# Attention in a fused transformer block: weighted values of two steps one behind the other, with four probability buffers

## The reference

```
x = x + 0.5 * moe(layernorm(x))          # 32 experts, top 8, capacity 128
x = x + attention(layernorm(x))
x = x + 0.5 * moe(layernorm(x))
# attention: 2 batches x 1024 tokens x 128 features, 16 heads of 8, rotary part of 32 common to the heads
c_kv = x @ W_kv_down
scores = (q . k + q_rope . k_rope) / sqrt(8 + 32), causal
attn = softmax(scores) @ v;   out = attn @ W_o
```

## Time and profile before

| | us |
|---|---|
| median of 3 runs | 605.45 (604.97 to 607.55) |
| profiled execution | 603.74 |
| its span | 601.7 |
| TensorE busy | 534.7 (89%) |
| VectorE busy | 425.6 (71%) |
| ScalarE busy | 259.8 (43%) |
| GpSimd busy | 89.3 (15%) |

### The profile page before, as it was taken

How to read it: one execution, slowest core, us unless ns; L and a number is a source line. 1 busy time by engine, 2 the same in 40 slices (tenths; PEclk the granted TensorE clock), 3 DMA queues, 4 the chain that set the end, 5 groups by cost and what they waited for, 6 DMA issues and landing times.

```text
span 601.7 us, 11027 instructions
## 1 busy us (share of the span) xinstructions
PE 534.7 (89%) x3522; PEld 332.9 (55%) x3546; DVE 425.6 (71%) x1423; ACT 259.8 (43%) x430; POOL 89.3 (15%) x208
## 2 busy tenths in 40 slices
PE   6869999969798999999999999999987875899995
PEld 2746767744464554555555555555533543577784
DVE  6966878774776776867678686767800895698973
ACT  2733212234544456465545646554577331121212
POOL 2500000011601121121212112121222140000000
PEclk9979999998997999999999999999999986899998
DMA  9964100000151000000000000000000620000002
GB/s 200 186 224 126 37 1 3 1 3 2 60 221 54 2 26 28 27 23 12 24 27 26 28 28 23 12 23 27 0 2 1 172 65 1 1 3 1 2 3 70
DMA packets 25094, 26.70 MB, mean 44 GB/s; under 512 B 6704, under 2 KB 18576, under 8 KB 25040
## 3 DMA queue, kind: packets, MB, share of 16 engines
q1 hardware_dynamic: 24176, 25.63, 15.1%
q10 hardware_dynamic: 864, 0.36, 0.2%
HBM read 17.04 MB, written 8.78 MB: 43 GB/s over the span
## 4 chain that ended last, share of the span: by engine, by line
PE 64%; DVE 23%; issue 6%; ACT 5%; DMA 1%; DVEq 0%; SPq 0%; POOL 0%; ACTq 0%
PE ps L1520 13%; PE ps L1585 12%; PE ps L1558 10%; PE ps L1236 7%; PE ps L1335 5%; PE ps L1320 4%; DVE onehot L880 3%; DVE mxh L1078 3%; PE ps L1516 2%; DVE summed L1075 2%; DVE place L954 2%; PE ps L1348 2%; DVE xn L804 2%; ACT probs L717 2%; DVE stats L780 1%
## 5 line engine op out<-in xcount | busy, mean ns | idle before, releaser
L717 ACT ACTIVATE probs<-ps 128x1024 f32<-128x1024 f32 (+2 forms) x192 | 148.2, 809 | 118.0 <-PE ps L1558 117.9
L1078 DVE TENSOR_REDUCE mxh<-ps 128x1 f32<-128x512 f32 (+2 forms) x176 | 117.4, 689 | 48.1 <-PE ps L1520 46.0
L1520 PE MATMUL ps<-Kst,Qst 120*128 120x512 f32 (+3 forms) x384 | 132.7, 412 | 7.0 <-DVE mxh L1078 3.9
L1520 PEld LDWEIGHTS ps<-Kst,Qst 120*128 120x128 f32 x384 | 67.1, 192 | 64.1 <-DVE mxh L1075 23.3
L1558 PE MATMUL ps<-Qst,Kst 121*128 121x512 f32 (+3 forms) x384 | 96.1, 356 | 1.9 <-ACT probs L717 1.7
L1075 DVE CUSTOM_DVE_ANT_0 summed<-ps,maskf 128x384 f32<-128x384 f32 (+1 forms) x128 | 76.0, 620 | 22.3 <-PE ps L1520 20.5
L1236 PE MATMUL ps<-onehot,xp 128*128 128x512 bf16 (+1 forms) x250 | 70.0, 407 | 17.1 <-DVE onehot L880 15.9
L490 POOL TENSOR_SCALAR_AFFINE_SELECT probs<-probs 128x256 f32<-128x256 f32 x128 | 52.1, 407 | 222.1 <-ACT probs L717 221.5
L1585 PE MATMUL ps<-probs,Vst 128*32 128x512 f32 (+3 forms) x768 | 82.4, 501 | 1.2 <-POOL probs L490 1.2
L1558 PEld LDWEIGHTS ps<-Qst,Kst 121*128 121x128 f32 x384 | 67.2, 191 | 22.6 <-ACT probs L717 7.3
L880 DVE TENSOR_SCALAR onehot<-iotab,posm 128x128 bf16<-128x128 bf16 (+1 forms) x352 | 63.0, 254 | 2.3 <-issue 2.0
(11 more groups left out here) (179 smaller groups left out, 607.2 us busy)
## 6 DMA issues: line engine op xcount, KB each, us to landing
wgn<-in_L_ffn_gate_up_proj SPq DMA_DIRECT2D x8, 384.0 KB, 6.2
guT_d<-gus SPq DMA_DIRECT2D x6, 384.0 KB, 3.1
gus<-guT_d SPq DMA_DIRECT2D x6, 384.0 KB, 6.2
Kst<-kn_d SPq DMA_DIRECT2D x28, 64.0 KB
Qst<-qn_d SPq DMA_DIRECT2D x28, 64.0 KB
wdn<-in_L_ffn_down_proj SPq DMA_DIRECT2D x8, 192.0 KB, 6.7
dnT_d<-dns SPq DMA_DIRECT2D x6, 192.0 KB, 3.5
dns<-dnT_d SPq DMA_DIRECT2D x6, 192.0 KB, 7.4
```

The source lines that it names most:

```text
L717: e.activation(probs[n % RING][:, 2 * b:2 * b + 2, lo:BANK], ps[:, 2 * b:2 * b + 2, lo:BANK], ACT.Exp, scale=SCALE).then_inc(probs_ready, 1)
L1078: e.tensor_reduce(to, s.rearrange("p (q k) -> p q k", k=w), AX.X, ALU.max).then_inc(mx_ready, 1)
L1520: ins = e.matmul(ps[:, bank, i * w:(i + 1) * w], Qst[p][h][0:ROWS, column(b, jt * P):column(b, jt * P) + P], Kst[p][h][0:ROWS, column(b, o ...
```

## The change

The weighted values are no longer issued in each step: in the odd steps those of the even step before and of the step itself are issued one directly behind the other (`BURST = 2`). The third and fourth quarters of the share stay in every step, behind them. There are four probability buffers (`PRING`). Three of them lie where `nh` and `nl` lie, so ScalarE waits before its first exponential until all stores of these are done. `SHARE` is set anew; its sum stays 38, and its entries for steps 1, 2, 3, 4, 8 and 10 change.

```diff
--- before.py
+++ after.py
@@ -80,7 +80,9 @@
 
 
 
-SHARE = [4, 3, 4, 3, 4, 3, 4, 4, 3, 3, 3, 0]
+SHARE = [4, 4, 3, 4, 3, 3, 4, 4, 2, 3, 4, 0]
+BURST = 2
+PRING = 2 * BURST
 LASTU = max(n for n in range(NS) if SHARE[n])
 LATE = OPENS[1]
 TH = BANK // P
@@ -231,8 +233,11 @@
         ord_ = sb("ord", [P, 4, 4], F32, att)
 
 
-        nh = [sb(f"nh{u}", [P, BANK], F32R, att) for u in range(NB)]
-        nl = [sb(f"nl{u}", [P, BANK], F32R, att) for u in range(NB)]
+        parting = ExitStack()
+        nh = [sb(f"nh{u}", [P, BANK], F32R, parting) for u in range(NB)]
+        nl = [sb(f"nl{u}", [P, BANK], F32R, parting) for u in range(NB)]
+        parting.close()
+        probs = [sb(f"probs{p}", [P, 4, BANK], F32, att) for p in range(PRING - 1)]
         ckvT = sb("ckvT", [D, N], F32, att)
 
         pre = ExitStack()
@@ -244,7 +249,7 @@
         ll = [sb(f"ll{s}", [P, BANK], F32R, pre) for s in range(2)]
         pre.close()
 
-        probs = [sb(f"probs{p}", [P, 4, BANK], F32, att) for p in range(RING)]
+        probs += [sb(f"probs{p}", [P, 4, BANK], F32, att) for p in range(PRING - 1, PRING)]
         oS = [sb(f"oS{j}", [P, BANK], F32, att) for j in range(2)]
         att.close()
         attn = xn
@@ -486,7 +491,7 @@
                     lo = kt * P - j * BANK
                     for b in range(B):
                         e.wait_ge(probs_ready, pair * 2 * NS + 2 * n + b + 1 + RING)
-                        block = probs[n % RING][:, 2 * b:2 * b + 2, lo:lo + P]
+                        block = probs[n % PRING][:, 2 * b:2 * b + 2, lo:lo + P]
                         e.affine_select(block, block, [[0, 2], [1, P]], ALU.is_ge, zero, base=0, channel_multiplier=-1).then_inc(masked, 1)
                     if n == DIAG[2] and pair + 1 < NPAIR:
                         stage_values(pair + 1, 1 - p)
@@ -707,14 +712,17 @@
 
 
             def pair_step(pair, p, half, first=False):
+                if first:
+                    for u in range(2 * NC):
+                        e.wait_ge(nope_stored[u], 32)
                 for n, (j, kt) in enumerate(STEPS):
                     lo = max(0, kt * P - j * BANK)
                     for b in range(B):
                         e.wait_ge(scores_done, pair * 2 * NS + 2 * n + b + 1)
                         if b == 0:
 
-                            e.wait_ge(pv_done, (pair + 2) * NS + n + 1 - RING)
-                        e.activation(probs[n % RING][:, 2 * b:2 * b + 2, lo:BANK], ps[:, 2 * b:2 * b + 2, lo:BANK],
+                            e.wait_ge(pv_done, (pair + 2) * NS + n + 1 - PRING)
+                        e.activation(probs[n % PRING][:, 2 * b:2 * b + 2, lo:BANK], ps[:, 2 * b:2 * b + 2, lo:BANK],
                                      ACT.Exp, scale=SCALE).then_inc(probs_ready, 1)
                     if n == 0 and not first:
                         copy_values(pair - 1, 1)
@@ -1582,12 +1590,10 @@
                         e.wait_ge(attn_ready, pair * 2 + j + 1)
                     for q in range(4):
                         b, h = q // 2, q % 2
-                        ins = e.matmul(ps[VW * q:VW * (q + 1), 4 + j, lo:BANK], Vst[p][:, b * TB + kt, h, :], probs[n % RING][:, q, lo:BANK],
+                        ins = e.matmul(ps[VW * q:VW * (q + 1), 4 + j, lo:BANK], Vst[p][:, b * TB + kt, h, :], probs[n % PRING][:, q, lo:BANK],
                                        start=(n == OPENS[j]), stop=(n == CLOSES[j]), skip_group_check=True)
                         if q == 3:
                             ins.then_inc(pv_done, 1)
-                    unit(n, 2, 4)
-                    unit(n, 3, 4)
 
                 for n in range(NS):
                     if n == 1 and not first:
@@ -1609,7 +1615,11 @@
                         scores(pair + 1, 1 - p, 0)
                     if n == LASTU + 1 and not last:
                         turn_maxima(pair + 1, 1)
-                    weighted(n)
+                    if n % BURST == BURST - 1:
+                        for m in range(n + 1 - BURST, n + 1):
+                            weighted(m)
+                    unit(n, 2, 4)
+                    unit(n, 3, 4)
 
             e.wait_ge(shift_in[0][0], 32)
             scores(0, 0, 0)
```

## The result

| | before | after |
|---|---|---|
| median of the runs, us | 605.21 (604.14 to 607.55, 4 runs) | 615.82 (614.96 to 616.00, 4 runs) |
| ratio, 95% interval | | 1.0155 (1.0123 to 1.0187) |
| profiled execution, its span | 603.74, 601.7 | 615.94, 614.2 |
| TensorE, VectorE, ScalarE busy | 534.7, 425.6, 259.8 | 538.2, 424.1, 259.1 |

All figures are of executions in the chip's usual state, except that e8's profile, like two of its ten executions, fell in a slower one.

The account below looks back on a forecast made before the run. TensorE sets the pace, but not alone: maxima scores have two PSUM banks, which VectorE empties. Seven pairs at 0.91 (6.4) plus last pair 0.4, rounded to 6.7, on 603.74 profiled, plus 1.7 to the median: 612 us, range 601.5 to 618.5.

Parts of the forecast that it names:

- the eight waits: ScalarE, before its first exponential: waiting for eight stores costs 0, with 9 us of cover; at most 0.5 us.
- Joint of two weighted steps: TensorE, odd steps: a weighted step followed by another takes 0.86 us instead of 0.99; bounds 0.853 and 1.00.
- Added waits for VectorE: TensorE's maxima units in a pair: waits rise 1.75 to 4.11 us; net with joints and weight loads +0.91.
- Rival B: Weighted steps: nothing gained at the joint, two take 2.0 us as apart; 618.5 us; chance 0.12.
- The rule of 1.28 us per bank: Maxima units, two PSUM banks: a unit starts no earlier than 1.28 us after the unit two before it.
- My own working of step 10: Step 10 of the new order, walked unit by unit: units 34, 36 and 37 wait 0.83 us in sum.
- I'm wrong if units in even steps start less than 1.28 us after their bank was last filled: Maxima units of even steps: earlier starts than 1.28 us after their bank's last filling would refute the prediction.
- Shares: Maxima units per step: new shares alone gain 0.3 us a pair; with old shares bursts cost 1.4 a pair.
- first exponential within 0.5 us of 189.70: ScalarE, start of attention: the first exponential should still start within 0.5 us of 189.70 in the trace after.
- Last pair: The last pair, without maxima, ScalarE against TensorE: +0.4 us, bounds -1.4 and +1.2.
- Rival A: Even steps: units wait no more than now, VectorE catches up, only savings remain; 591 us; chance 0.12.
- Rival C: TensorE's clock: many short waits make it fall once or twice more, up to 3.4 us each; 615.5 to 619; chance 0.07.

Follow-up runs that it names:

- e8: The changed kernel with shares 4 4 2 4 3 4 4 4 2 4 3 0, the walk's best for bursts: 607.45 us, 0.9986 times the kernel before.
- e5: The kernel before, with VectorE reducing only the first sixteenth of each maxima unit's columns: 586.36 us, 0.9618 times the kernel before.
- e6: The changed kernel, with VectorE reducing only the first sixteenth of each maxima unit's columns: 586.07 us, 0.9630 times the kernel before.
- e1: The kernel before with the new shares alone, weighted values in each step and two buffers: 606.08 us, 0.9981 times the kernel before.
- e2: The changed kernel with the old shares, so bursts without the new shares: 619.85 us, 1.0198 times the kernel before.
- e3: The changed kernel without bursts and with the old shares, keeping four buffers and the eight waits: 608.25 us, 1.0016 times the kernel before.
- e4: The changed kernel with a small exponential on ScalarE ahead of the eight waits, loading the table early: 614.06 us, 1.0114 times the kernel before.

## Why the prediction was right

I said 612.0 (601.5 to 618.5), 6.7 us slower; it was 615.8, 10.6 slower. That is inside the range but 0.8 us above the band of 607 to 615 that I gave 0.54. The mechanism, more waiting for VectorE than the joints save, was right in the middle pairs, which make up most of the sum; one smaller term, the eight waits, was wrong.

*Joint of two weighted steps.* Forecast 0.86 + 0.78 for the first burst, measured 1.64; forecast 1.85 for two full steps, measured 1.85. Rival B falls.

*Added waits for VectorE.* Forecast +0.91 us net in a pair, measured +1.04 to 1.09 (and +1.6 for the old shares against 1.4). The rule of 1.28 us per bank holds within 0.01 for units 34 and 36, whose banks were last filled behind a burst or a wait, but not as the lower bound that I stated: unit 37 starts 1.18 us after unit 35, as another in step 6 does (327.88), and the kernel before has 1.22. My own working of step 10 had 1.16 for unit 37, so the sign "I'm wrong if units in even steps start less than 1.28 us after their bank was last filled" contradicted it; the sign came true, and it refutes the figure as a bound for every unit, not the waiting. The term was 0.15 us too small, 1 us in six pairs. TensorE's shown waits came to 10.4 us, just below the 12 to 20 that I named: the view hides more of each than the 0.1 that I allowed. The middle pair of 36.11 lies just above the 35.9 to 36.0 that I named. e5 and e6 show the cause, since the difference of the pairs goes with VectorE's time.

*Shares.* I put them at a gain of 0.3 us a pair by themselves; e1 shows none. Their worth with bursts, 0.5 a pair (e2 against after), was forecast right.

*Buffers and the eight waits.* "0, with 9 us of cover" is the step that failed. The stores were indeed done long before; what stands behind them now is the table load, which had been hidden at 183.94, ahead of the first scores. I had counted what the waits wait for and not what they push behind them on ScalarE. The first pair was 1.9 us longer in e3, and e4 got 1.6 back. My mark "first exponential within 0.5 us of 189.70" had to be read from the first scores: before it starts 1.01 us after them, after 2.66 us.

*Last pair.* +0.4 forecast, +0.63 measured.

*Sum of attention.* Forecast 6.7; measured 9.2 = 6.5 (middle) + 2.0 (first) + 0.6 (last). The missing 2.5 us are 1.1 in the middle pairs, 1.1 in the first pair beyond its share of 0.91, 0.2 in the last, and rounding (6.4 and 0.4 are 6.8, which I rounded down). The other 1.4 of the 10.6 are not explained; in view of the 187.45 to 192.79 at which attention begins, whatever the kernel, and of medians of the kernel before of 605.21, 607.00 and 608.48 on three occasions, they need no cause in the change. The split of the first pair is not firm: bursts alone added 0.9 us there (e2 against e3), and only 0.4 with the new shares and the table early (e4 against before).

*Rival A* (bursts win since VectorE catches up) falls with e2 and after; its condition, a bank free in less than about 0.9 us, was set up in e6 (units that wait start 0.68 to 0.69 us after the unit two before), and there the loss vanished but its gain of 1.87 us a pair did not come. *Rival C* falls for the pairs: the granted clock is 1.00 from 204 to 475 us. In the first pair the clock did cost 1.8 us more (5.2 against 3.4), but with the late table's gap, not with the many short waits that the rival named.

## What to carry to other kernels

Work of TensorE that another engine doesn't have to follow is also that engine's time to empty its banks: moving it together saves tails and takes the spacing away. Before packing, take the time in which a bank comes free, walk the new order with it, and fit the shares to the order; here that alone gained 3.9 to 9.7 us (95% interval), while the packing with shares fitted to it came out even. When an explicit wait is put before an engine's first activation of a kind, look what hidden one-time work, like a table load, it moves behind the wait.

## What the runs showed of the hardware that I had not expected

Two weighted steps of four column tiles each run into each other almost without a seam: 1.64 us against 1.77 apart, 1.85 for two full ones against 1.98. A table load of 1.28 us went with a first pair longer by 1.6 to 1.9 us: the gap that it made on TensorE came while the clock was at 1.2 GHz, and the clock took 5.2 of 14 us instead of 3.4. In e6, where the load also stood behind the scores but TensorE had a single gap of 2.17 us, the clock took 3.4.
